# Moving the gather of first-layer weights from SyncE's DMA queue to ScalarE's

## The reference

```python
# x (128 batches, 128 channels, 1024), L0 weights (200, 128, 128),
# L1 weights (8, 128, 128), bias (8, 128)
x = x + einsum('bct,bcd->bdt', x, L0_weights[itok_B_1_198])
x = x + einsum('bct,bcd->bdt', x, L1_weights[itok_B_0_7]) + bias[itok_B_0_7][:, :, None]
```

## Time and profile before

| | |
|---|---|
| median of 3 runs | 347.73 us |
| profiled execution, its own time | 348.84 us |
| span of its trace | 347.1 us |
| PE busy | 266.8 us (77%) |
| VectorE busy | 126.3 us (36%) |
| ScalarE busy | 96.9 us (28%) |
| GpSimd busy | 65.3 us (19%) |
| mean granted TensorE clock | 0.961 |
| HBM read and written | 76.03 MB and 67.11 MB |

### The profile page before, as it was taken

The page is one execution under the profiler, slowest core; times in us unless marked ns, Lnnn a source line. Parts: engine busy times, 40 slices in busy tenths (PEclk is TensorE's granted clock), DMA queues, the critical chain, the costliest instruction groups (busy, mean ns, idle before and its releaser), DMA issues.

```text
span 347.1 us, 5157 instructions
## 1 busy us (share of the span) xinstructions
PE 266.8 (77%) x774; PEld 129.5 (37%) x774; DVE 126.3 (36%) x202; ACT 96.9 (28%) x135; POOL 65.3 (19%) x249
## 2 busy tenths in 40 slices
PE   1799991986798896979877779777679877778980
PEld 1344450442344442434433334433334433333430
DVE  3254541333334242433433344333334333334440
ACT  1133350221333133332232232422242222323230
POOL 2400222112221112221122212122221212221000
PEclk9999997899989898998999999999999999999996
DMA  7999969999999999999999999999999999999994
GB/s 306 410 409 393 378 248 351 424 418 397 417 431 415 433 423 427 417 416 427 432 425 427 427 423 432 421 436 423 419 431 425 432 430 426 423 421 440 419 405 171
DMA packets 24058, 140.80 MB, mean 406 GB/s; under 512 B 2673, under 2 KB 14322, under 8 KB 15474
## 3 DMA queue, kind: packets, MB, share of 16 engines
q1 hardware_dynamic: 23760, 140.20, 97.9%
q10 hardware_dynamic: 290, 0.53, 0.4%
HBM read 76.03 MB, written 67.11 MB: 412 GB/s over the span
## 4 chain that ended last, share of the span: by engine, by line
DMA 56%; SPq 27%; issue 9%; PE 5%; ACT 0%
DMA out<-xy 47%; SPq L127 10%; DMA xy<-x 9%; SPq L122 7%; PE y_ps L306 5%; SPq L128 4%; SPq L142 3%; SPq L145 2%; ACT xy L402 0%; PE m_ps L287 0%; SPq L159 0%; SPq L148 0%; SPq L153 0%; SPq L163 0%; SPq L154 0%
## 5 line engine op out<-in xcount | busy, mean ns | idle before, releaser
L306 PE MATMUL y_ps<-xy,m_sb 128*128 128x512 f32 x512 | 245.5, 616 | 61.3 <-DMA xy<-x 60.3
L306 PEld LDWEIGHTS y_ps<-xy,m_sb 128*128 128x128 f32 x512 | 92.9, 196 | 164.9 <-issue 164.9
L402 ACT ACTIVATE xy<-y_ps,j_pick 128x512 f32<-128x512 f32 x128 | 87.9, 687 | 233.1 <-PE y_ps L306 233.1
L378 DVE TENSOR_SCALAR xy<-y_ps,j_pick 128x512 f32<-128x512 f32 x128 | 96.1, 751 | 156.5 <-PE y_ps L306 156.5
L238 POOL COPY w_pick<-w_home 128x128 f32 x112 | 32.8, 293 | 245.4 <-issue 245.4
L287 PEld LDWEIGHTS m_ps<-j_pick,w_pick 128*128 128x128 f32 x224 | 35.4, 199 | 28.7 <-issue 28.7
L370 DVE TENSOR_TENSOR m_sb<-m_ps,j_pick 128x256 f32<-128x256 f32 x64 | 27.1, 424 | 45.2 <-PE m_ps L287 44.6
L287 PE MATMUL m_ps<-j_pick,w_pick 128*128 128x128 f32 x224 | 35.1, 281 | 0.0
L240 POOL COPY j_pick<-j_all 128x129 f32 x112 | 33.0, 295 | 0.1
L402 ACT ACT_TABLE_LOAD x7 | 9.0, 1283 | 7.9 <-POOL j_pick L252 7.8
L287 PE MATMUL m_ps<-j_pick,w_home 128*128 128x128 f32 x32 | 5.5, 297 | 6.7 <-DMA w_home<-w_t 6.7
(11 more groups left out here) (16 smaller groups left out, 2.8 us busy)
## 6 DMA issues: line engine op xcount, KB each, us to landing
xy<-x SPq DMA_DIRECT2D x30, 2048.0 KB, 15.1
out<-xy SPq DMA_DIRECT2D x29, 2048.0 KB, 13.4
w_home<-w_t SPq DMA_DIRECT2D x128, 64.0 KB
out<-xy SPq DMA_DIRECT2D x5, 1024.0 KB, 6.8
xy<-x SPq DMA_DIRECT2D x3, 1024.0 KB, 7.8
xy<-x SPq DMA_DIRECT2D x4, 256.0 KB, 12.6
j_all<-w_bias SPq DMA_DIRECT2D x1, 516.0 KB, 3.7
out<-xy SPq DMA_DIRECT2D x2, 256.0 KB, 5.1
```

The source lines that it names most:

```text
L306: nc.tensor.matmul(y_ps[:, b % YB, h, :], m_sb[:, s, k, :], xy[:, s, k, half(h)], start=True, stop=True).then_inc(y_ready, 1)
L378: nc.vector.tensor_scalar(xy[:, s, k, half(0)], y_ps[:, b % YB, 0, :], j_pick[:, s, k, D:D + 1], None, ALU.add).then_inc(left_out[b % YB], 1)
L402: nc.scalar.activation(xy[:, s, k, half(1)], y_ps[:, b % YB, 1, :], ACT.Identity, bias=j_pick[:, s, k, D:D + 1]).then_inc(right_out[b % YB ...
```

## The change

ScalarE gets the helpers for w0 loads. It waits for home_ready before its loop, and after the two evictions of pair s in round r (0 to 6) it calls load_w0(r + 1, s). The loads go on ScalarE's own DMA queue. SyncE loses all its load_w0 calls and its wait for home_ready; it keeps round 0's w0 loads, x and the stores, in the order in which they were.

```diff
--- before.py
+++ after.py
@@ -133,14 +133,6 @@
                 for k in range(PAIR):
                     load_one(s * PAIR + k, s, words[k], None)
 
-            def load_w0(r, s):
-
-                sp.wait_ge(w0_loaded[s], r * (PAIR * 16))
-                b = r * ROUND_B + s * PAIR
-                words = words_of(load_words[0:1, bass.ds(b, PAIR), :].rearrange("o b f -> o (b f)"))
-                for k in range(PAIR):
-                    load_one(b + k, s, words[2 * k], nc.s_assert_within(words[2 * k + 1], 0, 1))
-
             def load_quad(r, q):
                 sp.dma_start(slots(q), quad_of(x, r, q)).then_inc(x_loaded[q], 16)
 
@@ -166,10 +158,6 @@
             def load_quad_again(r, q):
                 sp.wait_ge(stored[q], stored_once(r, q))
                 load_quad(r, q)
-
-            def load_w0_of(r, q):
-                for s in range(q * QUAD, (q + 1) * QUAD):
-                    load_w0(r, s)
 
             sp.dma_start(j_all[:].rearrange("c n d -> c (n d)"), w1_bias.rearrange("c n d -> c (n d)"))\
               .then_inc(w1_loaded, 16)
@@ -183,24 +171,17 @@
                     load_quad(0, q + 1)
 
 
-            sp.wait_ge(home_ready, 4)
-            load_w0_of(1, 0)
             for s in range(QUAD + 1):
                 store_pair(0, s)
             load_quad_again(1, 0)
-            load_w0_of(1, 1)
             store_pair(0, QUAD + 1)
             with sp.Fori(1, ROUNDS - 1) as r:
                 for q in range(1, QUADS + 1):
                     now = (r, q) if q < QUADS else (r + 1, 0)
-                    after = (r, q + 1) if q + 1 < QUADS else (r + 1, q + 1 - QUADS)
-                    load_w0_of(*after)
                     store_quad(*((r, q - AHEAD) if q >= AHEAD else (r - 1, q - AHEAD + QUADS)))
                     load_quad_again(*now)
 
             for q in range(1, QUADS):
-                if q < QUADS - 1:
-                    load_w0_of(ROUNDS - 1, q + 1)
                 store_quad(*((ROUNDS - 1, q - AHEAD) if q >= AHEAD else (ROUNDS - 2, q - AHEAD + QUADS)))
                 if q < QUADS - 1:
                     load_quad_again(ROUNDS - 1, q)
@@ -393,6 +374,24 @@
 
         @block.scalar
         def _(act):
+            def words_of(words):
+                return nc.values_load_multi_w_load_instructions(
+                    words, engines=(mybir.EngineType.Activation,),
+                    skip_runtime_bounds_check_because="each word is checked against its own range below")[1]
+
+            def load_one(b, s, i, needed):
+                act.dma_start(w0_home[:, bass.ds(b, 1), :].rearrange("k b c -> k (b c)"),
+                             w0_t[bass.ds(nc.s_assert_within(i, 0, N0 - 1), 1), :, :].rearrange("n k c -> (n k) c"),
+                             cond=needed).then_inc(w0_loaded[s], 16)
+
+            def load_w0(r, s):
+
+                act.wait_ge(w0_loaded[s], r * (PAIR * 16))
+                b = r * ROUND_B + s * PAIR
+                words = words_of(load_words[0:1, bass.ds(b, PAIR), :].rearrange("o b f -> o (b f)"))
+                for k in range(PAIR):
+                    load_one(b + k, s, words[2 * k], nc.s_assert_within(words[2 * k + 1], 0, 1))
+
             def right(r, s, k):
 
                 b = s * PAIR + k
@@ -403,10 +402,12 @@
                                      bias=j_pick[:, s, k, D:D + 1]).then_inc(right_out[b % YB], 1)
 
             act.dma_start(cond_words[:].rearrange("o f b -> o (f b)"), cond).then_inc(cond_loaded, 16)
+            act.wait_ge(home_ready, 4)
             with act.Fori(0, ROUNDS - 1) as r:
                 for s in range(RING):
                     for k in range(PAIR):
                         right(r, s, k)
+                    load_w0(r + 1, s)
             for s in range(RING - 1):
                 for k in range(PAIR):
                     right(ROUNDS - 1, s, k)
```

## The result

The changed kernel takes 351.27 us (median of 20 runs, 348.19 to 354.09) against 348.02 for the kernel before (20 runs, 347.19 to 350.03). The ratio is 1.0088, with a 95% interval of 1.0068 to 1.0108: 0.9% slower, where 344.1 and "faster" were forecast. The ratio leaves out two of the 20 runs of the changed kernel, which were over 1.5% above its fastest; the median of the other 18 is 350.85. The profiled execution took 353.13 us with a span of 351.4.

The account below looks back on a forecast made before the run. DMA traffic of 140.80 MB was taken as the bound, except in a hole made by SyncE's issue time. Filling it gains 3.6 us, all other terms 0: median 347.73 becomes 344.1 us, range 340.5 to 348.0.

Parts of the forecast that it names:

- The hole: DMA engines partly empty at 44 to 60 us, ready stores behind w0 loads on SyncE; filling it gains 3.6 us.
- The walk of the queue: SyncE's transfers followed from the start: every issue precedes the queue running empty; narrowest at pair 5, 3.0 us of cover.
- Calls on ScalarE: 56 w0 calls between evictions, 3.2 us each (3.1 to 4.2); ScalarE keeps PE's pace, cost 0.
- ScalarE becomes the bound: Rival: slow calls of 4.8 us make ScalarE's period 5.5 us a pair; about 365 us, chance 0.09.
- They go on another queue: w0 loads on ScalarE's queue run up to a round ahead of GpSimd's picks, so none is late; no cost priced.
- another hole behind 50 us: Sign of being wrong: a further stretch of empty DMA engines, above all at the store of quad (1,0).
- Bytes and rate: Moving w0's 5.0 MB on a second queue: gain between 0 and 11.8 us, loss up to 10.9; taken as 0.
- interleaving slows the big transfers: Rival: full-stage rate falls from 424 to 408 GB/s, costing 10.9 us against the 3.6 gained; 355 us, chance 0.07.
- The rule of the Trainium skill: DMAs from different engines interleave on the same 16 engines; several issuers save only issue time; by it, about 0 gain.

Follow-up runs that it names:

- order_first: The kernel before, with SyncE's stores put ahead of the w0 loads only at the start and in the loop's first step: 345.05 us (0.992).
- round0: The kernel before, with ScalarE issuing only the w0 loads of round 1's pairs 2 to 5, during round 0: 345.08 us (0.993).
- rows4k_act: The changed kernel with x and out in 4 KB pieces: 349.81 us (1.006 of before); the kernel before with such pieces took 356.57.
- half: The changed kernel, but ScalarE issues only the odd pairs' w0 loads and SyncE the others: 343.50 us (0.987 of the kernel before).
- threequarter: The changed kernel, but SyncE issues the w0 loads of the first pair of each four, ScalarE the others: 343.75 us (0.987 of before).
- half_first: half and order_first together in one kernel: 344.40 us (0.989 of the kernel before).
- nomove_act: The changed kernel with all 56 calls issued on ScalarE but no w0 byte of rounds 1 to 7 moved: 328.62 us (0.945 of before).

## Why the prediction was wrong

- *The hole is SyncE's issue order, worth 3.1 to 5.1 us, taken as 3.6.* Right in place and nearly in size: 3.0 us by order_first and round0. The walk of the queue held at the start: first store near 39 (40.27), share 1.03. Only the first load came 3.1 us later than the walk had it (46.60 for 43.5).
- *Calls on ScalarE cost 3.2 us each and 0 on the path.* Right as far as ScalarE's own time goes: rows4k_act does them all at full length and gains 6.8 us. The forecast's rival "ScalarE becomes the bound" is refuted in its mechanism (slow calls), though ScalarE did stand still, for another reason: a queue that was behind.
- *"They go on another queue, up to a round ahead of GpSimd's picks: they can't be late."* **This is the step that failed.** A lead of a round, some 40 us, is a statement on latency. What was missing is the throughput of the second queue beside the first: one packet of 512 B per packet of 16 KB, 5.1 us a load, 10.2 a pair, against 5.1. While all loads move, a lead is used up at 5.1 us a pair, a round's lead in 8 pairs. It was gone by the load issued at 53.97, for which GpSimd waited until 94.68. The prediction had listed "another hole behind 50 us" among the signs of being wrong; it came at 90 to 105.
- *Bytes and rate.* I bounded what two queues could do to the big transfers, and that bound was not needed: at 180 to 300 us the rate is 424 for 427. The harm fell on the small ones. The rival "interleaving slows the big transfers" was priced at 355 by a wrong mechanism and given 0.07; no rival held the right one.
- *The rule of the Trainium skill.* I cited the Trainium skill for "interleave" and used it for the total rate only. Its account of how (packets in turn), in the section "Queues, rings and completion order" of the same page, with the packet sizes, would have led to the 1 to 1.

The rows ahead of the prediction had the means: two packet sizes can be read from the page's counts and the tile shapes, and the earlier trace rows has 24058 packets in all with 14322 under 2 KB. 128 packets of w0 against 128 of a quad was to be seen; that they go one for one was not, but it was the case to price.

## What to carry to other kernels

Moving small-row transfers to a queue of their own beside a saturated queue of long rows does not give them priority; it gives them one packet per long packet. Before such a move, divide the packets that the small queue will need by those that the big queue will send in the same stretch: below 1 it keeps up (in the traces 576 to 1574 in half, 886 to 1553 in threequarter, 1008 to 3544 with 4 KB rows), above 1 the trace shows 1 to 1, and any lead is only a delay of the loss. And when a hole comes from issue order, the cheapest cure is to reorder the one queue at that place.

## What the runs showed of the hardware

- Two DMA queues of one core, 16 KB and 512 B packets: 989 packets each in 35 us, 12.9 GB/s for the small one beside 411 for the big one.
- A queue that is behind can block its issuer: single issues of 7.6 and 11.2 us on ScalarE, where 0.35 is usual, and none over 0.60 in the runs in which it kept up (0.60 in round0, 0.45 in half_first).
- Packets of 4 KB in place of 16 KB for x and out cost 2.5% of this kernel's time (356.57 us beside 347.75).
- A single execution can lie about 1% over the median of its kernel, the profiled one too: nomove_act 333.17 for 328.62, half 346.8 for 343.50, and round0 347.98 for 345.08 in one that was not profiled.
